# Two more windows' maxima products between the halves of the second MLP product in a fused two-layer transformer kernel

## What is computed

```python
# layer 0, 16 heads of 16 channels; sh/sc/g: nine modulation rows per batch
h = _ln(x) * (1 + sc_msa) + sh_msa
x = x + self_attention_in_windows_of_128(h) * g_msa      # shifted by 64 tokens
h = _ln(x) * (1 + sc_mca) + sh_mca
x = x + cross_attention_top16_of_64_keys(h, context) * g_mca
h = _ln(x) * (1 + sc_mlp) + sh_mlp
u = h @ w_m1 + b_m1
x = x + (silu(u[..., :1024]) * u[..., 1024:] @ w_m2 + b_m2) * g_mlp
# layer 1: 16 heads, 64 keys, plain softmax
xq = (1 + scale) * _ln(x) + bias
out = softmax(q(xq) @ k.T / 4) @ v
return x + (out @ Wp + bp)
```

## Time and profile before

| what | value |
|---|---|
| runs | median 1017.48 us of 3 (1014.0 to 1018.24) |
| profiled execution | 1021.65 us; span on the core 1019.4 us |
| PE | busy 899.5 us, 88% |
| DVE | busy 753.6 us, 74% |
| ACT | busy 476.6 us, 47% |
| POOL | busy 218.6 us, 21% |
| mean granted TensorE clock | 0.962 |
| starts of `project(3, b)` in the six `full(a)` | 223.94, 337.48, 449.86, 563.23, 675.60, 787.97 us |

### The profile page before, as it was taken

One profiled execution on the slowest core, in us unless ns is written; L12 is line 12 of the kernel. 1 busy time (PEld: TensorE's weight loads), 2 busy tenths in 40 slices (PEclk: granted clock), 3 DMA queues, 4 the chain that ended last, 5 costly groups with the idle time before them and its releaser, 6 DMA issues.

```text
span 1019.4 us, 22231 instructions
## 1 busy us (share of the span) xinstructions
PE 899.5 (88%) x8152; PEld 654.4 (64%) x8152; DVE 753.6 (74%) x3953; ACT 476.6 (47%) x797; POOL 218.6 (21%) x164
## 2 busy tenths in 40 slices
PE   6977553999899989999899989998999988898997
PEld 4754441687567756687658756786568755674775
DVE  3646875799569985898769985898679964996423
ACT  3336323634566264634465264635574365434313
POOL 1015401402032130412041131402040222220101
PEclk9999785999999999999999999999999999897999
DMA  8250000000010102000010102000100101000000
GB/s 326 104 171 11 2 17 25 17 2 2 2 58 1 50 5 73 18 1 2 22 37 1 53 2 74 18 1 2 42 17 2 53 1 33 1 1 2 21 1 21
DMA packets 29067, 32.96 MB, mean 32 GB/s; under 512 B 4336, under 2 KB 26016, under 8 KB 28704
## 3 DMA queue, kind: packets, MB, share of 16 engines
q1 hardware_dynamic: 28960, 31.55, 9.5%
HBM read 25.19 MB, written 6.36 MB: 31 GB/s over the span
## 4 chain that ended last, share of the span: by engine, by line
PE 66%; DVE 21%; ACT 7%; issue 3%; POOL 1%; DMA 1%; SPq 0%; ACTq 0%; POOLq 0%
PE bank L1424 62%; DVE left L1136 6%; DVE negm L1099 5%; DVE top L1134 4%; PE bank L1593 2%; PE bank L1442 2%; ACT hT L730 2%; DVE negm L1161 1%; ACT arena L841 1%; DVE x L1073 1%; DVE stats L1035 1%; DVE arena L1128 1%; ACT rden_self L775 1%; DVE xh L1047 1%; DMA w_m<-in_w_ada 1%
## 5 line engine op out<-in xcount | busy, mean ns | idle before, releaser
L654 POOL TENSOR_TENSOR eS<-arena,top 128x1024 f32<-128x1024 f32 x32 | 61.9, 1936 | 291.4 <-DVE top L1134 291.4
L1424 PE MATMUL bank<-w_m,arena 128*128 128x256 f32 x512 | 112.6, 381 | 2.4 <-issue 2.4
L1424 PEld LDWEIGHTS bank<-w_m,arena 128*128 128x128 f32 x512 | 96.6, 190 | 16.8 <-issue 3.2
L1136 DVE MATCH_REPLACE8 left<-top,left 128x64 f32<-128x64 f32 x512 | 100.4, 237 | 0.0
L1136 DVE MATCH_REPLACE8 left<-top,arena 128x64 f32<-128x64 f32 x512 | 100.0, 225 | 0.0
L784 ACT ACTIVATE arena<-bank 128x512 f32<-128x512 f32 x128 | 66.1, 603 | 58.5 <-PE bank L1424 58.5
L830 ACT ACTIVATE rden<-bank,chan 128x512 f32<-128x512 f32 x64 | 44.1, 688 | 98.7 <-PE bank L1424 86.2
L617 POOL TENSOR_SCALAR veps<-mv 128x4 f32<-128x4 f32 (+1 forms) x32 | 7.9, 246 | 363.3 <-DVE mv L1042 363.2
L1134 DVE MAX8 top<-arena 128x8 f32<-128x64 f32 x512 | 67.9, 220 | 21.2 <-ACT arena L804 21.2
L1424 PE MATMUL bank<-qr,w_m 128*128 128x512 f32 x256 | 81.9, 401 | 0.2 <-ACT qr L740 0.2
L1099 DVE TENSOR_REDUCE negm<-bank 128x4 f32<-128x512 f32 x128 | 78.9, 685 | 3.8 <-PE bank L1424 3.0
(11 more groups left out here) (148 smaller groups left out, 1879.3 us busy)
## 6 DMA issues: line engine op xcount, KB each, us to landing
w_m<-in_w_m SPq DMA_DIRECT2D x4, 1024.0 KB, 5.7
xin<-in_x SPq DMA_DIRECT2D x4, 512.0 KB, 4.3
arena<-in_w_m SPq DMA_DIRECT2D x1, 2048.0 KB, 13.2
out<-x SPq DMA_DIRECT2D x4, 512.0 KB, 2.9
arena<-in_w_ada SPq DMA_DIRECT2D x1, 1536.0 KB, 10.9
gate<-gate_rows SPq DMA_DIRECT2D x12, 128.0 KB, 3.8
gated_bias<-gate_rows SPq DMA_DIRECT2D x12, 128.0 KB, 4.0
xin<-in_x SPq DMA_DIRECT2D x4, 384.0 KB, 3.2
```

The costliest lines, as they stand in the source:

```text
L654: nc.gpsimd.tensor_tensor(eS[:], S[:, t, :].rearrange("p (h n) -> p h n", h=H), top[:, :, 0:1].to_broadcast([P, H, LC]), ALU.subtract).the ...
L1136: i = nc.vector.match_replace(left[:, h, :], eight, scores, REPLACED)
L1424: return nc.tensor.matmul(dst, lhsT, rhs, start=start, stop=stop)
```

## The change

In PE's `full(a)` the products of windows 2 and 3 move from behind `window(a, 0)` and `window(a, 1)` to a place between y0 and y1; `bank_order()` follows. DVE takes the maxima of windows 2 and 3 there too, and its top-k steps are dealt out anew behind them; in front of the second `window_max(a, 3)` stand the moments of the first half. `cross_divide(4, b)` is split, with step 3 of the fourth tile between its halves. On ACT the fourth tile's exponential moves behind `self_denominator(a, 1)`. No operation is added or removed. The wait for the last weights in a = 2 moves ahead of `window_values(a, 0)`.

```diff
--- before.py
+++ after.py
@@ -72,8 +72,8 @@
             yield ("D", layer, n, k)
             yield ("O", layer, n, k)
 
-    def project(layer, n):
-        for u in range(2):
+    def project(layer, n, halves=(0, 1)):
+        for u in halves:
             yield ("y", layer, n, u)
 
     def scores(n, halves=(0, 1)):
@@ -162,11 +162,12 @@
         yield from mlp_in(b)
         for w in range(2):
             yield from by_row_group("A", a, w)
-        yield from project(3, b)
+        yield from project(3, b, (0,))
+        for w in range(2, W):
+            yield from by_row_group("A", a, w)
+        yield from project(3, b, (1,))
         yield from window(a, 0)
-        yield from by_row_group("A", a, 2)
         yield from window(a, 1)
-        yield from by_row_group("A", a, 3)
         yield ("PV", a, 0)
         yield from by_chunk("T", 4, b)
         yield from window(a, 2)
@@ -930,8 +931,8 @@
                 modulated(4, b)
                 window(a, 2)
                 last_query(b)
+                self_denominator(a, 1)
                 topk_exp(c, 3)
-                self_denominator(a, 1)
                 window(a, 3)
                 self_denominator(a, 2)
                 last_exps(b)
@@ -1071,6 +1072,11 @@
                 tiles = slice(2 * u, 2 * u + 2)
                 src = xin[:, tiles] if layer == 1 else x[:, slot, tiles]
                 drain(nc.vector.tensor_tensor(x[:, slot, tiles], ps(key).rearrange("p (t n) -> p t n", t=2), src, ALU.add), key)
+
+            def half_moments(layer, n, u):
+
+                drained_wait(dve, ("y", layer, n, u))
+                moments_of(layer + 1, x[:, n % SLOTS], range(2 * u, 2 * u + 2))
 
             def residual_moments(layer, n, halves=(0, 1)):
 
@@ -1315,23 +1321,28 @@
                         topk(c, 1, (j,))
                 window_max(a, 0)
                 window_max(a, 1)
-                topk(c, 2, (0, 1))
-                residual_moments(3, b, (0,))
-                topk(c, 2, (2, 3))
+                topk(c, 2, (0,))
+                residual(3, b, 0)
+                window_max(a, 2)
+                half_moments(3, b, 0)
+                window_max(a, 3)
                 residual_moments(3, b, (1,))
-                window_max(a, 2)
+                topk(c, 2, (1,))
                 normalise(4, b, (3, b))
-                window_max(a, 3)
-                topk(c, 2, (4,))
+                topk(c, 2, (2,))
                 window_divide(a, 0)
-                topk(c, 3, (0, 1))
+                topk(c, 2, (3, 4))
+                topk(c, 3, (0,))
                 window_divide(a, 1)
                 last_max(b)
+                topk(c, 3, (1,))
+                window_divide(a, 2)
                 topk(c, 3, (2,))
-                window_divide(a, 2)
-                topk(c, 3, (3, 4))
-                cross_divide(4, b)
+                cross_divide(4, b, (0,))
+                topk(c, 3, (3,))
+                cross_divide(4, b, (1,))
                 window_divide(a, 3)
+                topk(c, 3, (4,))
                 residual(4, b, 0)
                 residual(4, b, 1)
                 residual_moments(1, a)
@@ -1802,14 +1813,15 @@
                 mlp_in(b)
                 scores_for_max(a, 0)
                 scores_for_max(a, 1)
-                project(3, b)
+                project(3, b, (0,))
+                scores_for_max(a, 2)
+                scores_for_max(a, 3)
+                project(3, b, (1,))
                 window(a, 0)
-                scores_for_max(a, 2)
                 window(a, 1)
-                scores_for_max(a, 3)
-                window_values(a, 0)
                 if a == 2:
                     pe.wait_ge(s_wlast, 32)
+                window_values(a, 0)
                 transposed(4, b)
                 window(a, 2)
                 last_query(b)
```

## The result

The changed kernel takes 1035.35 us, the median of 4 runs (1030.83 to 1037.94), beside 1016.17 us before (1014.0 to 1018.24): ratio 1.0184, 95% interval 1.0139 to 1.0229. It is slower by 19 us. Its profiled execution took 1036.53 us with a span of 1034.3 us, 14.9 us more than the span before. The two profiles account for these 14.9 us and not for the other 4.3: the profiled execution of the kernel before, 1021.65 us, was itself slower than its four timed runs.

A forecast was written before the change was run, and what follows sets the result against it. PE's list, with places where PE waits for DVE, was taken to bound the kernel. Order +10.8 us and clock falls +5.0 gave +15.8 on 1017.5, 1033.3, forecast as 1033, range 1023 to 1039.

The forecast's parts named there:

- the order: Whole block: late division after the front's surviving gain costs 1.8 us a block, +10.8 us in six.
- the clock: PE at project(4, b): three clock falls in six blocks behind the long wait, 1.66 us each, +5.0 us.
- The front: PE from second MLP product to turn of xh: 0.77 us a block won of 1.81, turn at 22.65.
- the two new waits on ACT: PE waits about 0.7 us ahead of window 1's products and 0.8 us ahead of its subtraction.
- the list of PE's gaps: PE's idle gaps of 0.88, 0.57 and 0.36 us, 1.81 us a block, as what a reordering could win.
- other edits I cost at nothing: Bank order behind window 2, reload of second MLP weights and the wait in a = 2: no cost.
- The split division: DVE's step 3 between the halves delays project(4, b): +1.8 us a block after the 0.5 gain.
- surviving gain: At the last maxima, 0.5 us a block of the front's 0.77 remains after waits on ACT.
- The rival that the clock falls in every block: Late division with a fall in five or six blocks: 1036.6 to 1038.3 us, chance 0.17.
- Faster: PE's three front gaps all go and the split costs nothing: 1006.6 us, chance 0.05.
- no difference: Split costs as forecast but the front wins the whole 1.81 us: 1020.5 us, chance 0.07.
- The fifth: DVE misses normalise, the turn of xh waits up to 1 us, another +6: 1039 us, chance 0.05.

The follow-up runs named there:

- e2: Changed kernel with window_divide(a, 2) moved ahead of step 1 of the fourth tile, the split kept: 1025.38 us, ratio 1.010.
- e3: Kernel before with only the split of the last division added, step 3 between the halves and step 4 after window_divide(a, 3): 1032.26 us, ratio 1.0164.
- e5: Changed kernel with window_divide(a, 2) ahead of step 1 and both halves of the last division together ahead of step 3: 1010.67 us, ratio 0.9964.
- e7a: e5 plus ACT copying window 1's maxima after window 0's first exponential, and DVE's third-tile steps 1 and 2 moved earlier: 1013.89 us, ratio 0.9962.
- e1: Changed kernel with the split undone, step 3 of the fourth tile ahead of both divisions: 1018.10 us, ratio 1.0028.
- e9: Changed kernel plus four filling matmuls, result overwritten, in PE's wait ahead of project(4, b): 1028.80 us, ratio 1.0117.
- e6: e5 plus only ACT copying window 1's maxima right behind window 0's first exponential, DVE's order left: 1006.61 us in one run.
- e10_short: e7a plus filling matmuls, result overwritten, in the two short PE waits at the last scores: 1003.87 us, ratio 0.9898.
- e11_start: e10_short with GpSimd's subtraction splitting the first MLP weights cut from two operations of 128x2048 into eight of 128x512: 1004.45 us.

## Why the prediction was right, point by point

**The time and its two terms.** 1033 was forecast and 1035.35 measured; on the profiled execution 1037.4 and 1036.53. The sum had +10.8 for the order and +5.0 for the clock; the traces show +12.6 and +4.0, and 1.7 us less in the start and the end, which the forecast did not have. So the total is closer than its terms, and that is luck. It is luck too that +15.8 on the first three runs' 1017.5 comes within 2.4 us of the median: that median rose by 19.2 over the 1016.17 of four runs.

**The front.** The gaps ahead of both maxima products are gone, the two new waits on ACT are there at 0.50 and 0.40 us (about 0.7 and 0.8 forecast), DVE idles 2.61 us for y1 (2.5 forecast) and makes normalise in time. The turn of xh was forecast at 22.65 and is at 22.75, the last maxima at 35.65 and 35.50. This was the long part of the working and it held within 0.15 us. What it left out: the list of PE's gaps as 1.81 us a block stops at window 3's maxima products. Behind them the kernel before waits 0.25, 0.74, 0.36, 0.69 and 0.76 us more, and the last of these waits is the one that grew.

**The step that failed**, though the forecast held, is the one that said "other edits I cost at nothing: order of banks behind window 2 is unchanged". The order of banks is, but not the time at which one of them comes free: `window_divide(a, 2)` had moved behind step 1 of the fourth tile, it drains the bank that the last scores' third product of the second half takes eight places later, and PE waited 1.44 us there instead of the 0.77 that e2 shows and the 0.76 of the kernel before. That took 0.67 us a block, the whole gain of the front. I had that division in my sum of DVE's steps, as 0.4 us of work ahead of the last division, and never asked who waits for it. e2 shows it by itself.

**The split division** was right in kind and 0.2 us too dear: it costs 2.07 us by e3, 2.3 forecast, because PE starts 0.05 us behind the division, not 0.25, and the step between the halves takes 3.10 us, not 3.20. DVE idles 2.89 us ahead of the first division, 2 forecast: it comes 0.3 us earlier, and the inverse 0.6 later through the wait for the bank. Forecast 2.3 less 0.5 of surviving gain, 1.8; measured 2.06 less nothing, 2.1. The two errors go against each other and leave 0.3 us a block.

**The clock.** Three falls of 1.66 us were forecast behind the wait; three came, at 1.68 to 1.69, in the profiled run. That the number is just three is luck: two gaps were all that the forecast had to go by. What the term left out: two more falls beside the last scores, of whose cost the long wait behind them hides a part and leaves 0.75 and 0.26 us, and the 2.1 us that two falls cost in the kernel before and that have to be taken off. One of those stands beside its last scores (1.16 us), the other 18 us behind Y in a = 4, beside the gaps of 0.88 and 0.57 us, of which the change removes the first and leaves 0.50 of the second (0.99 us). The prediction saw these two blocks only as "the same within 1.2 us". The rival that the clock falls in every block is not borne out: a = 5 has the same wait of 1.99 us and no fall. The rule of the Trainium skill (TensorE: Matmul & The Clock Gate, HAM oscillation) that a repeated wait can throttle the array in each round anew holds for half the rounds here and in e3, and for one in six in e2.

**The other rivals.** Faster (1006.6) and no difference (1020.5) needed the front to win 1.81 us a block; it wins 0.62, and 1.18 with the copy and DVE's step mended. The fifth, a late normalise, did not come up.

## What to carry to other kernels

When a step is put between two halves of something on a strictly ordered engine, add it to the second half's time and look at who waits for that half; 3.1 us of top-k between two divisions that had started 1.3 us apart cost 2.1 us of TensorE six times. For every instruction that changes place, ask for the bank it frees as well as for the value it makes. A reordering that seems to give nothing can be a good one with two bad companions: undo the parts one at a time and read offsets inside one repeated block, where 0.1 us can be read, before the whole run's time.

## What the runs showed of the hardware

**The clock also falls beside short waits.** In e2, e5 and e7a the granted clock fell eight times in eighteen blocks at the last scores, beside waits of 0.69 and 0.77 us among small matmuls, at 1.0 to 1.2 us a time. In e1 and e9, where the second of the two waits is 1.44 to 1.53 us, it fell six times in twelve, at 0.8 to 2.7 us. Filling the short ones with matmuls whose result is overwritten cost 0.05 us a block, and no fall came in twelve. e6 had none in six unfilled, so a short wait does not always bring one; whether it is the wait or the small matmuls round it, no run here separates.

**One of two things happens at about 102 us.** In the start of the kernel one DVE operation with two tensor operands, the masking of 128x1024, meets the seam between two GpSimd operations of 4.5 us. DVE's and GpSimd's lines in the changed kernel:

```profile
101.28 5.84 DVE L1134 SCALAR_TENSOR_TENSOR arena<-left,eS 128x1024 f32<-128x1024 f32 x1
96.97 9.07 POOL L674 TENSOR_TENSOR m_low<-arena,w_m 128x2048 fp32r<-128x2048 f32 x2 [6.25 <-ACT w_m L896]
```

and in e10_short:

```profile
100.15 1.27 DVE L1146 SCALAR_TENSOR_TENSOR arena<-left,eS 128x1024 f32<-128x1024 f32 x1
95.84 10.00 POOL L674 TENSOR_TENSOR m_low<-arena,w_m 128x2048 fp32r<-128x2048 f32 x2 [6.25 <-ACT w_m L907]
```

Either DVE takes 1.27 us and GpSimd's pair 10.0 us, or DVE takes 5.84 and GpSimd 9.07, as if the one that comes first holds the other back. The profiles of before, after, e7a and e9 have the long one, all others of the table but the last the short one. The difference of the masking is 4.6 us, as much as several edits here are worth, and e7a's profile had the long one and e5's not. From the masking's start to the first of the six blocks it is 119.9 to 121.6 us in the four and 115.2 to 116.9 in the seven. It is not the whole spread: the masking itself starts anywhere from 100.2 to 103.9 us, and up to 1.7 us more differ behind it. e11_start cuts the pair into eight:

```diff
-                nc.gpsimd.tensor_tensor(m1_low[:, k, :], m1_in[:, k, :], w_m1[:, k, :], ALU.subtract).then_inc(s_m1_split, 1)
+                for at in range(0, 2 * HID, BT):
+                    cut = slice(at, at + BT)
+                    i = nc.gpsimd.tensor_tensor(m1_low[:, k, cut], m1_in[:, k, cut], w_m1[:, k, cut], ALU.subtract)
+                i.then_inc(s_m1_split, 1)
```

> The best kernel so far plus one edit in the start, which has nothing to do with the change: GpSimd's subtraction that splits the first MLP weights, two operations of 128x2048 (4.5 us each), is cut into eight of 128x512. In five profiles DVE's first masking (two tensor operands, 128x1024) meets the seam of the two: it took 1.27 us and GpSimd's pair 10.0 us in two of them, 5.8 to 5.9 us and 9.1 in three, and the six blocks began at 217 to 218 in the first and 223 to 225 us in the others. My theory: DVE waits for the GpSimd operation that came first, so the masking now takes at most 2.5 us, the six blocks begin at 217 to 219 us in every run, and the runs spread by less than 3 us around 1001 to 1005. Rival (the seam is not the cause): a masking of 5.8 us still comes up and the runs spread as before, by 5 us or more.

```profile
101.74 1.72 DVE L1149 SCALAR_TENSOR_TENSOR arena<-left,eS 128x1024 f32<-128x1024 f32 x1
97.42 10.85 POOL L676 TENSOR_TENSOR m_low<-arena,w_m 128x512 fp32r<-128x512 f32 x8 [6.25 <-ACT w_m L910]
```

The masking took 1.72 us and the blocks began at 218.3 us. Six runs lay within 3.3 us (1002.88 to 1006.15), a little more than expected, while ten runs of the kernel before beside them spread over 9.7 us. But other sets of runs of that kernel were narrower, nineteen beside e1 within 4.5 us and seven beside e10 within 3.6, so six runs prove little. It is not faster than e10_short (1003.0 to 1005.19), whose four runs may all have had the short one; that the seam causes the two lengths fits all profiles, but only one profile shows the pieces.
